# Two early products for the maxima moved within the chunks of a first layer, and a first sum split into a copy and a sum

## What is computed

```python
# layer 0
q, k, v = Wq@xf + bq, Wk@xf + bk, Wv@xf + bv          # 32, 32 and 256 rows of 4096
scores = einsum('bci,bcj->bij', q, k)
attn = softmax(scores, axis=1)
out = gamma * einsum('bcn,bnm->bcm', v, attn) + xf
# layer 1, on the output of layer 0
theta = conv1x1(x, theta_w, theta_b)                   # 32 rows of 4096
phi, g = maxpool2(conv1x1(x, phi_w, phi_b)), maxpool2(conv1x1(x, g_w, g_b))   # 32 and 128 rows of 1024
attention = softmax(einsum('nid,ndj->nij', theta, phi), axis=-1)
out = gamma * conv1x1(g attended, out_w, out_b) + x
```

## Time and profile before

| | us |
|---|---|
| median of three runs (2714.31 to 2731.46) | 2717.7 |
| the profiled execution | 2717.54 |
| its span, first to last instruction | 2715.7 |
| TensorE busy | 2610.4 (96%) |
| VectorE, GpSimd, ScalarE busy | 2036.5, 1979.4, 1741.6 |
| mean granted TensorE clock | 0.986 of 2.4 GHz |

### The profile page before, as it was taken

The page is one execution under the profiler, slowest core; times in us unless marked ns, Lnnn a source line. Parts: engine busy times, 40 slices in busy tenths (PEclk is TensorE's granted clock), DMA queues, the critical chain, the costliest instruction groups (busy, mean ns, idle before and its releaser), DMA issues.

```text
span 2715.7 us, 38345 instructions
## 1 busy us (share of the span) xinstructions
PE 2610.4 (96%) x11632; PEld 2078.7 (77%) x11632; DVE 2036.5 (75%) x3351; ACT 1741.6 (64%) x3171; POOL 1979.4 (73%) x1546
## 2 busy tenths in 40 slices
PE   7999999989999999998999999999899999999988
PEld 6788788777678888887678888888667888888765
DVE  7678777767777777776777777787677777877665
ACT  5566666667756666666775666666676666666566
POOL 3677777767867777775886777777588777777668
PEclk9999999999999999999999999999899999999989
DMA  2000000012110000001220000000121000000011
GB/s 90 1 16 16 17 24 17 24 40 71 63 32 21 20 23 18 17 16 41 70 78 24 17 24 16 17 16 17 47 79 63 16 16 16 17 17 16 17 47 63
DMA packets 45552, 85.28 MB, mean 31 GB/s; under 512 B 5032, under 2 KB 5160, under 8 KB 45352
## 3 DMA queue, kind: packets, MB, share of 16 engines
q1 hardware_dynamic: 37720, 68.41, 7.6%
q10 hardware_dynamic: 7632, 14.42, 1.8%
HBM read 49.03 MB, written 33.55 MB: 30 GB/s over the span
## 4 chain that ended last, share of the span: by engine, by line
PE 78%; DVE 12%; issue 5%; ACT 2%; POOL 1%; DMA 1%; SPq 0%; ACTq 0%; POOLq 0%; DVEq 0%
PE o_ps L914 16%; PE o_ps L917 16%; PE o_ps L918 16%; PE s_ps L891 9%; PE aux L954 8%; DVE mx L740 5%; DVE acc L702 3%; PE aux L928 2%; PE aux L992 1%; PE aux L975 1%; PE aux L932 1%; DVE aux L781 1%; PE aux L971 1%; POOL prob_l L502 1%; ACT queries L589 1%
## 5 line engine op out<-in xcount | busy, mean ns | idle before, releaser
L502 POOL TENSOR_TENSOR prob_l<-prob,prob_h 128x512 fp32r<-128x512 f32 x1280 | 1665.7, 1309 | 628.5 <-ACT prob_h L564 622.2
L561 ACT ACTIVATE prob<-s_ps 128x512 f32<-128x512 f32 x1280 | 766.8, 599 | 781.9 <-PE s_ps L891 779.8
L740 DVE TENSOR_REDUCE mx<-aux 128x1 f32<-128x512 f32 x1097 | 749.0, 683 | 290.9 <-PE aux L954 285.6
L914 PE MATMUL o_ps<-prob_h,vh 128*128 128x512 f32 x2304 | 912.4, 396 | 0.7
L917 PE MATMUL o_ps<-prob_l,vh 128*128 128x512 f32 x2304 | 903.6, 392 | 2.5 <-POOL prob_l L502 2.2
L918 PE MATMUL o_ps<-prob_h,vl 128*128 128x512 f32 x2304 | 900.8, 391 | 0.0
L702 DVE TENSOR_TENSOR acc<-prob,acc 128x512 f32<-128x512 f32 x1152 | 790.1, 686 | 61.9 <-ACT prob L561 49.6
L564 ACT ACTIVATE prob_h<-s_ps 128x512 fp32r<-128x512 f32 x1280 | 764.4, 597 | 0.0
L891 PE MATMUL s_ps<-queries,keys 128*128 128x512 f32 x1280 | 514.8, 403 | 22.9 <-DMA queries<-nm_turned 11.6
L914 PEld LDWEIGHTS o_ps<-prob_h,vh 128*128 128x128 f32 x2304 | 434.7, 189 | 101.2 <-ACT osb L575 9.8
L917 PEld LDWEIGHTS o_ps<-prob_l,vh 128*128 128x128 f32 x2304 | 434.4, 189 | 101.1 <-POOL prob_l L502 11.6
(11 more groups left out here) (131 smaller groups left out, 1845.4 us busy)
## 6 DMA issues: line engine op xcount, KB each, us to landing
xa<-x SPq DMA_DIRECT2D x32, 512.0 KB, 3.7
spill<-xa SPq DMA_DIRECT2D x32, 512.0 KB, 2.7
xa<-spill SPq DMA_DIRECT2D x32, 512.0 KB, 3.7
y<-xa SPq DMA_DIRECT2D x32, 512.0 KB, 2.8
xp<-x ACTq DMA_DIRECT2D x26, 512.0 KB, 3.7
queries<-nm_turned SPq DMA_DIRECT2D x236, 1.0 KB
xp<-x SPq DMA_DIRECT2D x2, 512.0 KB, 9.5
prob<-w_in ACTq DMA_DIRECT2D x1, 640.0 KB, 5.9
```

Of the source, the lines that this page charges most:

```text
L502: nc.gpsimd.tensor_tensor(out=prob_l[:, i, :], in0=prob[:, i, :], in1=prob_h[:, i, :].bitcast(f32), op=ALU.subtract).then_inc(pl_ready, 1)
L561: nc.scalar.activation(prob[:, i, :], s_ps[s][:, :], ACT.Exp).then_inc(p_ready, 1)
L740: ins = nc.vector.tensor_reduce(out=dst, in_=bank[:, :], axis=AX.X, op=ALU.max)
L914: mm(o_ps[ct][:, :], value(vh, l, t, ct), prob_h[:, i, :], start=t == 0, stop=False)
```

## The change

For chunks n = 1 to 6 of layer 0 the products on X0 at steps 3 and 6 are left out of the list, and X1 gets two more, at steps 9 and 13. The first chunk of an image (n = 0) keeps the old list. The products stay 32; since they are numbered in the order of the list, the one at a given step is now of another block of keys, of equal size. In layer 1 the sum at `t == 1` of two slots gives way to a copy of `prob` into `acc` at `t == 0`, and at `t == 1` the same kind of sum as in all later steps. Layer 0 keeps its first sum.

```diff
             if n + 1 < NCH:
-                steps = sorted(([(t, 3 if t else 1, X0) for t in range(25)]
-                         + [(t, 1, X1) for t in (8, 11, 14, 22, 23, 24, 25)]), key=lambda e: e[:2])
+                steps = sorted([(t, 3 if t else 1, X0) for t in range(25) if n == 0 or t not in (3, 6)]
+                               + [(t, 1, X1) for t in ((8, 9, 11, 13, 14) if n else (8, 11, 14)) + (22, 23, 24, 25)], key=lambda e: e[:2])
...
                     if (h, A) in LAST_ON:
                         wait_free(dve, LAST_ON[h, A])
-                elif t == 1:
+                    if l:
+                        nc.vector.tensor_copy(acc[:, :], prob[:, i, :]).then_inc(acc_done, 1)
+                elif t == 1 and l == 0:
                     nc.vector.tensor_tensor(out=acc[:, :], in0=prob[:, (h - 1) % RING, :], in1=prob[:, i, :],
                                             op=ALU.add).then_inc(acc_done, 2)
```

## The result

The changed kernel takes 2702.41 us in the median of seven runs (2700.23 to 2706.74), against 2721.54 of seven runs of the kernel before: the ratio is 0.9931, with an interval of 0.991 to 0.9952. That is 19 us less (13 to 24 by the interval); 22 were forecast, as 2695.5 against 2717.5. So it lies inside the range, and the change is within 1%, as expected. Of the two parts only the first was worth what its term said.

The account below looks back on a forecast made before the run. PE was taken to set the pace of layer 0. From 2717.5 us, 17 came off for the moved products and 5 for layer 1's copy and sum, giving 2695.5; range 2683 to 2710.

Parts of the forecast that it names:

- The wait at step 6 and its price: Layer 0, chunks 1 to 6: moving the products removes PE's wait for DVE's reduction, 0.70 us a chunk, 16.8 in all.
- Nothing is late next: Layer 0, step 7: the next product on X0 finds its bank free with 1.3 us of slack.
- rival 3: Layer 0: the wait moves to step 7 with half the loss, giving 2704.5 us; chance 0.13.
- The room in steps 9 and 14: Layer 0: nine matmuls take 2.04 us against DVE's 1.8, and X1 has been free for over a microsecond.
- Rival 4: Layer 0, steps 9 and 14: the product on X1 finds its bank held, giving 2732.5 us; chance 0.05.
- rival 2: Layer 1: the copy takes turns with POOL as the old sum did, costing 13 us, giving 2713.5; chance 0.12.
- The term of part 2: Layer 1, 32 chunks: copy and sum for one sum, 1.20 us replacing 1.17 on DVE, about -5 us in all.
- Long sums: Layer 1, some nine chunks with sums of 1.4 to 1.6: reciprocal 0.3 us earlier, PE's D2 0.2 earlier, -1.8 us.
- Short sums: Layer 1, some eight chunks with sums of 0.69: PE's D2 up to 0.1 us later, +0.8 us.
- GpSimd as the limit: Layer 1: POOL spared 0.43 a chunk; five chunks of image 3 give -2.2 us, six last chunks of other images -1.8.
- Rival 1: Layer 1: POOL's relief counts in full, -14 us in place of -5, giving 2686.5; chance 0.18.
- An earlier first sum: Layer 1, each image's first sum: the copy may run while DVE would have waited for the second probability, -0.5 to -1 us.

Follow-up runs that it names:

- part 1 alone: The kernel before with only the new list of products in layer 0, layer 1 keeping its old first sum: 2705.8 us, 0.9932 of before.
- e4: The kernel before with only the product of step 6 moved, to step 13, and the old sum in layer 1: 2707.7 us, 0.9941 of before.
- e2: The kernel before with only the copy and sum in layer 1, the old list of products in layer 0: 2719.2 us, 0.9982 of before.
- e11: The changed kernel with the copy written as a maximum of the slot with itself, reading two inputs: 2739.4 us, 1.0069 of before.
- e9: The changed kernel, unaltered, measured again: 2703.6 us, 0.9936 of before.
- e10: The kernel before with only the new list of products in layer 0, measured again: 2702.8 us, 0.9932 of before.

## Why the prediction was right, and where it was off

- **The wait at step 6 and its price.** Right in kind and size: 0.70 a chunk and 16.8 us were forecast; the 24 chunks went from 62.54 to 61.84 in the mean, 16.8 us, and part 1 alone measures 16.1 to 17.2. The step that paid was to read the loss from the distance of starts and not from the 0.39 of idle time that the view gives.
- **Nothing is late next.** Right on bank X0, to 0.1 us (rival 3 falls). The forecast treated the two moves as one; e4 shows that the one of step 6 does nearly all of it.
- **The room in steps 9 and 14.** Here the forecast was lucky. It took X1 to be free "for over a microsecond", since a reduction can start 0.43 after its product. It starts 1.17 after it (212.40 to 213.57), behind the reduction of product 7 and a sum, and 0.2 us of room is left. Rival 4 falls, as no product of chunk 1 waits (PE is busy all of its 61.80 us), but by 0.2 us and not by one.
- **The copy.** Its length was right (0.685 for 0.69) and rival 2 falls: in this kernel a copy from SBUF into PSUM doesn't take turns with GpSimd. In layer 1, 30 instructions L502 took over 1.5 us before (1.73 in the mean), and 3 do now. The Trainium skill says ("VectorE: DVE Perf Modes", Why PSUM operands drop a tier) that an operand in PSUM keeps 32-bit floats at the plain rate; the 0.685 us of the copy, beside 0.68 for a sum of the same size, agrees with it.
- **The term of part 2, -5.** This is the term that was mis-sized: on top of part 1 it is -0.4 to -1.6. What failed was "1.20 replaces 1.17: nothing on DVE". I put the copy and the sum 0.60 apart, but they depend on each other and start 0.78 apart, so the pair takes 1.39 up to the inversion. Piece by piece, from the chunks at full clock:
  - *Long sums, -1.8.* The inversion was to come 0.3 earlier. It had started 1.55 behind the start of the longest sum, and 1.37 behind those of 1.45 us. With 1.39 now only the fourth chunk of images 0 to 2 gains, 0.15 each: some -0.4.
  - *Short sums, +0.8.* PE loses 0.37 us in each seventh chunk of images 0 to 2, 0.3 in each third and in the second of image 3, where 0.1 had been taken: +2.3.
  - *GpSimd as the limit, -2.2 and -1.8.* The five windows of the earlier trace rows take 12.4, 12.4, 13.2, 13.2 and 11.5 us, together 1.2 less, where each was to lose some 0.4. The 0.3 a chunk for the last two chunks of images 0 to 2 did not come: the eighth stays at 11.9 with GpSimd now idle for 1.1 us there, so it wasn't the limit. Rival 1, which counted all of GpSimd's relief, falls: the relief came (3 long L502 in place of 30), but little of it reached PE.
  - *An earlier first sum, -0.5 to -1.* Not seen where it can be compared: the first chunk of image 0 takes 22.8 us before and in e2, at a granted clock of 0.92 in both.

  These pieces add up to about +1, the runs say -0.4 to -3; that difference is open. (The pieces as forecast add up to -5.5 to -6, not to the -5 of the sum.)
- **The sum.** -17 and about -1, so some -17.6 at equal clock; the median's -19 has a share of clock in it. 2695.5 was 7 us too low for 2702.4. About 4 of them are part 2. The rest is scatter: the profiled run of before from which I subtracted and the median run of the changed kernel both lay at a clock of 0.986, but 2717.5 is 1 us below four other runs of before at that clock (2718.3 to 2718.8), and 2702.4 is the highest of four of the changed kernel there (2700.2 to 2702.4).

## What to carry to other kernels

When an engine falls behind over some steps and then meets a wait, look for the one request that comes before the debt is paid; moving that one away was worth 16 us here, and lightening the load ahead of it 8. An instruction split in two does not cost twice the pitch of independent ones if the second reads what the first wrote (1.39 us here and not 1.20), and the pair should not stand ahead of something that another engine waits for. When a place gets a second job, follow the other engine's whole queue up to it, and not only its shortest reaction. A VectorE instruction with two inputs in SBUF beside a busy GpSimd had no fixed duration in these runs (0.69 to 5.26 us for the same work); the copy kept to 0.68 to 0.70 in all 32 chunks, and the sums with one input in PSUM to 0.64 to 0.70, whatever GpSimd did.

## What was not expected of the hardware

- A VectorE instruction that reads two tensors from SBUF can stand still through several GpSimd instructions in a row: 5.26 us for work of 0.69, with four L502 of 4.94 us in all (e11). In the kernel before the longest was 1.87.
- A sum on VectorE that reads the bank which the instruction ahead has written starts 0.78 us behind it; with an independent instruction between them the starts are 0.60 apart.
- The same kernel moves by 15 us (2714 to 2729) with the mean granted clock between 0.988 and 0.982. Pauses that a change adds can lower the clock itself: in e11 all six runs have 0.976 to 0.979, where the 23 runs of the other three kernels of its comparison (before, e9, e10) have 0.981 to 0.988, so its added pauses are paid twice. That shorter pauses raise the clock isn't shown.
